# A gated delta-rule layer with a Hadamard FFN: output-weight folding moved from GpSimd to VectorE, split Horner tiles, and new instruction orders

## The reference, cut to what matters

```
xn = layernorm(x)
qkvz = xn @ w_qkvz.T ; q, k, v through a causal convolution of 4 taps ; b, a = xn @ w_ba.T
g = -exp(A_log) * softplus(a + dt_bias) ; beta = sigmoid(b) ; q, k normalised
for each token t:                       # 32 heads of 64
    S = S * exp(g_t) ; delta = (v_t - k_t S) * beta_t ; S = S + k_t delta^T ; o_t = q_t S
o = o * rsqrt(mean(o^2) + eps) * norm_weight * sigmoid(z) ; y_attn = o @ w_out.T
h = fwht(xn * SU_ug) ; u = silu(h @ W_gate.T * s_g) * (h @ W_up.T * s_u)
y_ffn = (fwht(u * SU_dp)) @ W_down.T * Wscale_dp        # fwht of length 1024
out = x + y_attn + y_ffn
```

## Time and profile before

| | |
|---|---|
| median of 3 runs | 920.72 us (919.37 to 922.29) |
| the profiled execution | 921.86 us, span 920.0 us |
| PE busy | 845.0 us (92%), 13354 products and as many weight loads |
| DVE busy | 703.3 us (76%) |
| ACT busy | 256.0 us (28%) |
| POOL busy | 287.7 us (31%) |
| mean granted PE clock | 0.967 of full speed |
| DMA | 49.56 MB, mean 54 GB/s |

### The profile page before, as it was taken

The page is one execution under the profiler, slowest core; times in us unless marked ns, Lnnn a source line. Parts: engine busy times, 40 slices in busy tenths (PEclk is TensorE's granted clock), DMA queues, the critical chain, the costliest instruction groups (busy, mean ns, idle before and its releaser), DMA issues.

```text
span 920.0 us, 30578 instructions
## 1 busy us (share of the span) xinstructions
PE 845.0 (92%) x13354; PEld 607.2 (66%) x13354; DVE 703.3 (76%) x1248; ACT 256.0 (28%) x560; POOL 287.7 (31%) x194
## 2 busy tenths in 40 slices
PE   1887499999999999999999999999999999998685
PEld 1533267766767676767676677767777767767574
DVE  5675968888887979788887878797978888795522
...
GB/s 124 128 58 81 6 77 36 31 82 30 94 30 83 23 80 37 69 32 64 60 31 82 30 94 24 89 19 77 42 58 44 41 84 30 60 31 14 30 2 46
DMA packets 129157, 49.56 MB, mean 54 GB/s; under 512 B 110977, under 2 KB 120449, under 8 KB 128897
## 3 DMA queue, kind: packets, MB, share of 16 engines
...
...
## 4 chain that ended last, share of the span: by engine, by line
PE 60%; DVE 17%; SPq 7%; DMA 6%; POOL 5%; issue 3%; ACT 1%; POOLq 0%; DVEq 0%; ACTq 0%
PE bank L581 17%; DVE kq L224 4%; PE bank L645 4%; PE bank L593 3%; PE bank L747 3%; SPq L512 3%; PE bank L662 3%; PE bank L749 3%; PE bank L692 3%; PE bank L602 3%; PE bank L664 3%; PE bank L730 2%; PE bank L668 2%; PE bank L719 2%; PE bank L678 2%
## 5 line engine op out<-in xcount | busy, mean ns | idle before, releaser
L581 PE MATMUL bank<-xnT,wq 128*128 128x512 f32 x512 | 261.8, 636 | 15.8 <-DVE kq L224 15.5
L224 DVE SCALAR_TENSOR_TENSOR kq<-bank,cw,kq 128x510 f32<-128x510 f32 (+2 forms) x288 | 214.6, 745 | 44.9 <-ACT kq L798 37.8
L581 PEld LDWEIGHTS bank<-xnT,wq 128*128 128x128 f32 x512 | 90.7, 195 | 98.1 <-issue 70.3
L948 POOL TENSOR_TENSOR ost<-ost,cst 128x8 f32<-128x8 f32 x32 | 52.3, 1634 | 191.7 <-DVE ost L357 191.7
L798 ACT ACTIVATE kq<-bank,cw 128x512 f32<-128x512 f32 x96 | 65.8, 685 | 143.3 <-PE bank L581 142.5
L944 POOL TENSOR_TENSOR Sd<-St,dec 128x256 f32<-128x256 f32 x32 | 19.9, 621 | 231.7 <-DVE St L345 161.4
L938 POOL TENSOR_TENSOR kqg<-kq,rows 128x1024 f32<-128x1024 f32 x32 | 75.5, 2358 | 39.0 <-DVE kq L224 39.0
L645 PE MATMUL bank<-kq 64*64 64x128 f32 x1024 | 69.0, 274 | 11.6 <-DVE kq L224 8.9
L911 POOL TENSOR_TENSOR kd<-kc,stat 128x512 f32<-128x512 f32 x32 | 33.4, 1042 | 144.1 <-DVE stat L261 144.1
L747 PE MATMUL bank<-wo,oT 128*128 128x256 f32 x256 | 70.6, 389 | 1.6 <-DVE oT L369 1.6
L270 DVE TENSOR_TENSOR ATP<-bank,gb 128x512 f32<-128x512 f32 x64 | 44.1, 689 | 30.4 <-issue 14.3
...
## 6 DMA issues: line engine op xcount, KB each, us to landing
rows<-decay_rows SPq DMA_DIRECT2D x64, 256.0 KB, 4.6
...
inverse_blocks<-UU SPq DMA_DIRECT2D x16, 256.0 KB, 2.0
...
wguT<-wgu_dram SPq DMA_DIRECT2D x8, 256.0 KB, 5.2
base_blocks<-ATP SPq DMA_DIRECT2D x128, 16.0 KB, 2.7
...
U<-inverse_blocks SPq DMA_DIRECT2D x128, 16.0 KB, 2.0
```

The source lines that it names most:

```text
L224: nc.vector.scalar_tensor_tensor(out=y[:, :, t:S], in0=p[:, :, 0:S - t], scalar=cw[:, m, i // 2, 3 - t:4 - t], in1=y[:, :, t:S], op0=ALU.m ...
L581: last = nc.tensor.matmul(ring[i % 2][:], wq[:, q, kc, i // 2, :], xnT[:, kc, (i % 2) * 512:(i % 2) * 512 + 512], start=kc == 0, stop=kc = ...
L948: nc.gpsimd.tensor_tensor(ost[:, 2, :], ost[:, 1, :], k("neghalf")[:, 0:B * 2], ALU.pow).then_inc(rms_done, 1)
```

## The change

1. **Folding.** `fold()` on POOL is gone. `W_down` is loaded early, as SP's fourth transfer, into a tile of its own (a view of `kqg`, which the pairs use later); `Wscale_dp` comes first on ACT's queue. DVE multiplies by `Wscale_dp` (`wscaled`, 2 instructions on 128x1024) and does the three butterfly levels (6 instructions on 128x1024), all in the setup, ahead of PE's Hadamard product. The factor 1/sqrt(1024) goes into ACT's eviction of it. The first `out` waits for that eviction and not for the fold; POOL's first `kqg` waits until PE has read the tile.
2. **Clearings first.** POOL's four clearings stand ahead of its wait for the statistics.
3. **Small loads on ACT's queue.** `wsd`, `ah` (4 transfers) and `nwh` (2) are issued by ACT ahead of its first instruction.
4. **Horner by corner tiles.** `hz.1` multiplies only the two 32x32 diagonal corners of `Q` for each head (64 products of 32x32 by 48 columns for each pair, where there were 32 of 64x64 by 48); `hz.3` uses 64x32 of `Q` and writes 32 rows.
5. **New orders** on all engines and on SP's queue. `fload` stands ahead of `oload` in the setup.

```diff
-        wdT = xs
+        wds = [kqg[:, i].rearrange("p k u c -> p (k u c)").rearrange("p (i d) -> p i d", i=IT) for i in range(2)]
...
+                def butterfly(src, dst, h, t):
+
+                    s4, d4 = (w.rearrange("p (a t h) d -> p a t h d", t=2, h=h) for w in (src, dst))
+                    step(nc.vector.tensor_tensor(d4[:, :, t], s4[:, :, 0], s4[:, :, 1], (ALU.add, ALU.subtract)[t]))
+
+                def wscaled(i):
+
+                    step(nc.vector.tensor_tensor(wds[1][:, 4 * i:4 * i + 4], wds[0][:, 4 * i:4 * i + 4], wsd[:].unsqueeze(1).broadcast_to([P, 4, HID]), ALU.mult))
+
+                dve.wait_ge(wdn_in, 16)
+                dve.wait_ge(wsd_in, 16)
+                wscaled(0)
                 dve.wait_ge(sq_done, TT)
                 step(nc.vector.tensor_scalar(st[:, 0, :], st[:, 2, :], 1.0 / HID, LN_EPS, ALU.mult, ALU.add))
                 steps["var"] = count[0]
+                wscaled(1)
                 dve.wait_ge(rstd_done, 1)
...
                 for q in (1, 3):
+                    butterfly(wds[1], wds[0], 1, q // 2)
                     dve.wait_ge(xnT_ready, q + 1)
...
+                for t in range(2):
+                    butterfly(wds[0], wds[1], 2, t)
+                for t in range(2):
+                    butterfly(wds[1], wds[0], 4, t)
+                steps["fold"] = count[0]
...
DVE's order
-K.out.0 K.turn.1 K.out.1 M.e M.stats K.out.2 K.out.3 M.gram.0 L.hz.0.0 L.hz.0.1 M.gram.1 M.vtr.0 L.hz.1.0 L.hz.1.1
-M.gram.2 L.hz.2.0 L.hz.2.1 M.ff M.gram.3 L.hz.3.0 L.hz.3.1 A.proj.0 L.state.0 M.vtr.1 L.ks.1 A.proj.1 M.inv.0 L.state.1
-A.proj.2 L.ks.2 M.inv.1 L.norm.0 L.state.2 A.proj.3 L.ks.3 L.gated.0 M.inv.2 L.turn.0 L.norm.1 A.proj.4 L.gated.1
-A.proj.5
+M.hz.3.0 M.hz.3.1 A.vtr.1 P.proj.0 M.state.0 P.proj.1 M.ks.1 A.inv.0 P.proj.2 M.state.1 A.inv.1 M.ks.2 M.norm.0
+P.proj.3 M.state.2 M.gated.0 M.ks.3 A.inv.2 M.turn.0 P.proj.4 M.norm.1 P.proj.5 M.gated.1 M.out.0 M.turn.1 P.e P.stats
+M.out.1 M.out.2 P.gram.0 M.out.3 P.gram.1 A.hz.0.0 P.vtr.0 A.hz.0.1 A.hz.1.0 P.gram.2 A.hz.1.1 P.ff A.hz.2.0 A.hz.2.1
+P.gram.3
...
SP's order
-M.rload M.fload L.bout L.bin A.load L.uout L.uin L.oload
+K.bin L.rload M.load L.fload K.oload K.uout K.uin L.bout
...
PE, hz.1
+                        if j == 1:
+                            for rs, cs in ((top, slice(0, H2)), (low, slice(H2, C))):
+                                for h in range(2):
+                                    last = nc.tensor.matmul(M[H][rs[h], i * n:i * n + n], Q[rs[h], u, cs], U16[rs[h], u, C - n:C], start=True, stop=True)
+                            continue
...
PE, hz.3
-                                last = nc.tensor.matmul(M[H][hs[h], i * n + n - H2:i * n + n], Q[hs[h], u, :], X[hs[h], q, u, H2:C], start=True, stop=True)
+                                last = nc.tensor.matmul(M[H][top[h], i * n + n - H2:i * n + n], Q[hs[h], u, 0:H2], X[hs[h], q, u, H2:C], start=True, stop=True)
...
PE's order
-M.proj.4 K.ks.3 M.ktr.1 K.delta.3 K.turn.0 K.o.1 M.proj.5 K.out.0 K.out.1 M.proj.6 M.vtr.0 K.turn.1 M.proj.7 K.out.2
-K.out.3 M.ff L.hz.0.0 L.hz.0.1 M.gram.1 L.hz.1.0 L.hz.1.1 M.gram.2 L.hz.2.0 L.hz.2.1 M.gram.3 L.hz.3.0 L.hz.3.1
-A.proj.0 L.delta.0 M.vtr.1 L.state.0 A.proj.1 L.ks.1 M.qsq L.delta.1 A.proj.2 L.state.1 L.o.0 L.ks.2 A.proj.3 L.delta.2
-A.ktr.0 L.state.2 A.gram.0
+K.hz.1.0 L.gram.2 K.hz.1.1 K.hz.2.0 L.gram.3 K.hz.2.1 L.vtr.1 K.hz.3.0 K.hz.3.1 M.proj.0 K.delta.0 M.proj.1 K.state.0
+L.qsq K.ks.1 M.proj.2 K.delta.1 M.proj.3 K.state.1 K.o.0 M.ktr.0 K.ks.2 M.proj.4 K.delta.2 M.ktr.1 K.state.2 M.gram.0
+K.ks.3 K.turn.0 K.delta.3 M.proj.5 K.o.1 K.out.0 K.out.1 M.vtr.0 M.proj.6 K.turn.1 M.proj.7 K.out.2 M.ff K.out.3
+M.gram.1 L.hz.0.0 L.hz.0.1
...
ACT's order
-A.ktr.0 L.delta.3 A.proj.4 A.ktr.1 L.norm.1 A.proj.5 M.inv.2 A.proj.6 A.proj.7 A.ff A.qsq P.proj.0 M.delta.0 P.proj.1
-M.oload M.delta.1 A.qsum P.proj.2 M.norm.0 M.delta.2 P.proj.3 P.dec
+K.delta.2 M.proj.4 M.ktr.1 K.delta.3 L.inv.2 M.proj.5 K.norm.1 M.proj.6 M.proj.7 M.ff A.proj.0 M.qsq L.delta.0 A.proj.1
+A.proj.2 M.qsum L.delta.1 M.oload A.proj.3 L.norm.0 A.dec A.ktr.0
...
POOL's order
-P.kqg.0 P.kd.0 P.gb.0 P.root P.gb.1 P.kqg.1 A.sd.1 P.kd.1 A.sd.2 A.norm.0 A.norm.1
+A.gb.1 A.kd.0 A.kqg.0 A.kqg.1 M.sd.1 M.sd.2 A.kd.1 M.norm.0 M.norm.1 P.gb.0 P.root
```

More of the change, by code:

```diff
@@ L458, in _ @@
                 program({"proj": proj, "ff": ff, "e": e, "stats": stats, "gram": gram, "vtr": vtr, "inv": inv, "hz": hz, "ks": ks,
-                         "state": state, "norm": norm, "gated": gated, "turn": turn, "out": out}, """K.out.0 K.turn.1 K.out.1 M.e M.stats K.out.2 K.out.3 M.gram.0 L.hz.0.0 L.hz.0.1 M.gram.1 M.vtr.0 L.hz.1.0 L.hz.1.1
-                         M.gram.2 L.hz.2.0 L.hz.2.1 M.ff M.gram.3 L.hz.3.0 L.hz.3.1 A.proj.0 L.state.0 M.vtr.1 L.ks.1 A.proj.1 M.inv.0 L.state.1
-                         A.proj.2 L.ks.2 M.inv.1 L.norm.0 L.state.2 A.proj.3 L.ks.3 L.gated.0 M.inv.2 L.turn.0 L.norm.1 A.proj.4 L.gated.1
-                         A.proj.5""")
+                         "state": state, "norm": norm, "gated": gated, "turn": turn, "out": out}, """M.hz.3.0 M.hz.3.1 A.vtr.1 P.proj.0 M.state.0 P.proj.1 M.ks.1 A.inv.0 P.proj.2 M.state.1 A.inv.1 M.ks.2 M.norm.0
+                         P.proj.3 M.state.2 M.gated.0 M.ks.3 A.inv.2 M.turn.0 P.proj.4 M.norm.1 P.proj.5 M.gated.1 M.out.0 M.turn.1 P.e P.stats
+                         M.out.1 M.out.2 P.gram.0 M.out.3 P.gram.1 A.hz.0.0 P.vtr.0 A.hz.0.1 A.hz.1.0 P.gram.2 A.hz.1.1 P.ff A.hz.2.0 A.hz.2.1
+                         P.gram.3""")
                 dve.wait_ge(acc_done, PAIRS * 4)
@@ L545, in _ @@
                 sp.dma_start(cst[:, 0:at], consts[:, 0:at]).then_inc(const_in, 16)
+                sp.dma_start(wds[0], wdown).then_inc(wdn_in, 16)
                 sp.dma_start(wbas[:], wba).then_inc(gate_in, 16)
[L547 to L549 removed]
                 for v, src in ((su, su_ug), (sd_, su_dp), (wsu, ws_up), (wsg, ws_gate)):
@@ L662, in hz @@
                                 last = nc.tensor.matmul(dst, ATP[hs[h], q, u, 0, :], T16[hs[h], u, 0:n], start=True, stop=True)
-                            elif j == 1:
-                                last = nc.tensor.matmul(dst, Q[hs[h], u, :], U16[hs[h], u, C - n:C], start=True, stop=True)
                             elif j == 2:
@@ L773, in _ @@
                     last.then_inc(xh_ready, 1)
[L774 removed]
+                pe.wait_ge(v_step, steps["fold"])
                 for m in range(4):
                     pe.wait_ge(xh_done, m + 1)
[L777 removed]
+                    nc.tensor.matmul(spare[m][:], k("had"), wds[0][:, 2 * m:2 * m + 2, :], start=True, stop=True).then_inc(wd_ready, 1)
                 program({"proj": proj, "ff": ff, "ktr": ktr, "vtr": vtr, "qsq": qsq, "gram": gram, "hz": hz, "ks": ks, "delta": delta,
[L779 to L782 removed]
+                         "state": state, "o": o, "turn": turn, "out": out}, """K.hz.1.0 L.gram.2 K.hz.1.1 K.hz.2.0 L.gram.3 K.hz.2.1 L.vtr.1 K.hz.3.0 K.hz.3.1 M.proj.0 K.delta.0 M.proj.1 K.state.0
+                         L.qsq K.ks.1 M.proj.2 K.delta.1 M.proj.3 K.state.1 K.o.0 M.ktr.0 K.ks.2 M.proj.4 K.delta.2 M.ktr.1 K.state.2 M.gram.0
+                         K.ks.3 K.turn.0 K.delta.3 M.proj.5 K.o.1 K.out.0 K.out.1 M.vtr.0 M.proj.6 K.turn.1 M.proj.7 K.out.2 M.ff K.out.3
+                         M.gram.1 L.hz.0.0 L.hz.0.1""")
             @block.scalar
```

61 lines of the change are left out of this document (21 added, 40 removed).

## The result

The changed kernel takes 960.2 us (median of 4 runs, 956.0 to 969.4), the kernel before, run beside it, 920.8 (4 runs, 919.4 to 922.3): ratio 1.0441, interval 1.0363 to 1.052. I had forecast 933, with 908 to 945 as the range. The direction was right, the size missed by 27 us.

The account below looks back on a forecast made before the run. PE's own instruction sequence was taken to set the steady-state time: 921.9 - 2.0 - 15.5 + 14 x (0.96 + 1.0) + 3 = 934.8 us profiled, 933.7 by the runs, stated as 933; range 908 to 945.

Parts of the forecast that it names:

- Part 1: Setup: pair 0 begins 2 us earlier through faster normalising, 2 of 4 us charged for work ahead; bounds -4 and 0.
- Part 2: Filling up to pair 1's FFN product: -15.5 us, from earlier block stores and DVE products no longer stalled; bounds -17 and -11.
- the 12.5 us of stalled products: Filling: DVE's products of two SBUF operands, standing still while POOL folds, would give back 12.5 us.
- Part 3: PE's instruction sequence in the steady state: +0.96 us for each pair, 14 times, from shape changes, `hz.3` and `hz.1`.
- The shape changes: PE's sequence: nine more changes of tile shape a pair, 31 for 22, at 0.10 us each, +0.9 us.
- `hz.3` (-0.8): PE's sequence: 64x32 products should cost like 32x32, 1.13 us for 32 instead of 1.93, -0.8 us a pair.
- `hz.1`: PE's sequence: 64 corner products at 0.042 us take 2.7 us for 1.85 before, +0.86 a pair; bounds 2.1 and 3.7.
- Part 4: PE's waits for each pair: +0.3 at `turn.1`, +1.2 from a DVE-POOL collision, -0.5 old waits, together +1.0 us.
- The collision of `inv.1` with POOL: Steady state: DVE's SBUF products fall under POOL's pair and lose about 1.55 us, of which about 1.2 reach PE.
- rival A: Steady state: the DVE-POOL collision stays in DVE's room; period 51.0, time 916.8, faster than before; chance 0.33.
- Part 5: Tail after the last periods: +3 us, +1.8 from later `gram.3` and +1.2 from Horner steps; bounds 0 and +6.
- C: Rival on `hz.1`: four-corner products cost more, 0.058 us each, giving 947 us; chance 0.05.

Follow-up runs that it names:

- e1: Changed kernel, but SP's queue issues the output weights' load (`oload`) one period earlier, after `uin`; 925.4 us, ratio 1.0046.
- e5: Changed kernel with the output weights' load issued earlier on SP's queue and the old `hz.1` and `hz.3`; 917.2 us, ratio 0.9971.
- e3: Changed kernel with `hz.1` and `hz.3` of the kernel before; 937.1 us, ratio 1.0157.
- e12: Kernel before with the new setup and 64x32 `hz.3`, `wscaled` and first butterfly level moved behind the copies of `xnT`; 903.7 us, ratio 0.9836.
- e9: Kernel before with the new setup alone, all orders and Horner steps old; 910.3 us, ratio 0.9882.
- e13: Kernel before with the new setup and 64x32 `hz.3`, `bout` and `bin` put first on SP's queue; 899.2 us, ratio 0.9779.
- e6: Kernel before with only the 64x32 form of `hz.3`; 910.9 us, ratio 0.9901.
- e4: Kernel before with both new Horner steps, `hz.1` and `hz.3`, alone; 938.6 us, ratio 1.0173.
- e7: Kernel before with only the four-corner form of `hz.1`; 940.5 us, ratio 1.0219.

## Why the prediction missed

**What bounds the kernel.** Right: PE's sequence sets the period, and the sum splits as I had split it. e1, e5 and the kernel before part the 3.39 us a period: 53.63 - 51.58 = 2.05 late weights, 51.58 - 51.07 = 0.51 corner tiles, 51.07 - 50.24 = 0.83 order. The first two aren't additive: from the changed kernel, taking the corner tiles back first (e3, by its fastest run) gives 1.81, and the load then 0.75.

**Part 1, setup, -2.0.** Wrong by about 3: pair 0's FFN product comes at 67.70, where it came at 66.92 before, +0.8. (Over all traces it comes at 64.3 to 66.9 with the old setup and at 65.6 to 68.6 with the new one, 1.7 later in the mean.) The normalising fell to 2.67 us, but the first half of `x` landed at 6.93 (before: at 4.73), and I charged 2 us for what stands ahead of the variance where DVE's wait for `W_down` alone was 3.78. By e12 even that was off the path: the last folding steps, which I had put under the wait for the gates, delay the gates themselves.

**Part 2, filling, -15.5.** Right in size, 15.48. Of its two halves, the 12.5 us of stalled products can have given no more than the 10 of e9, of which part is the clock: over these 208 products PE is busy 35.5 us before and 32.7 in e9, at a mean granted clock of 0.78 and 0.85. That the stores' place on SP's queue gives 5 is not borne out: e13 has it in the old order without the gain. The other 5 are shorter waits of PE and a higher granted clock, as e9's rows show; what in the new order brings them stays open.

**Part 3, sequence, +0.96.** The shape changes (+0.9 for nine) are right in kind: the traces have 22 a period before and 31 after, as counted. e5 has only six of the nine and +0.83 a period with no more waiting, where 0.10 for each would make 0.6. `hz.3` (-0.8) is right: its group fell by 0.80, of which, with one more edge, 0.6 reaches the period in e6. `hz.1` is the mis-sized term. I reasoned that the first of a float32 product's two instructions must end before the second begins in that tile, 42 ns for both; they take 25.6, so 1.6 us a pair instead of 2.7, below my lower bound of 2.1. The term is -0.2 (twice 0.82 for 1.85; in e4's order, 1.49 for both halves, it is -0.4) and not +0.86. The 25 ns for each instruction that I had worked out from the Trainium skill, "TensorEngine Tiling (Array Packing)", section Instruction Overhead, lie further off still: the rows have 12.8. Then the same speed cost more than it gave, by a mechanism that I hadn't got: PE goes on with a new block of instructions only 2.2 to 3.6 us after its transfer starts, and 128 fast products don't last that long. The corner form of `hz.1` costs 1.2 us a period in the old order (e7); both new steps together cost 0.5 in the new one (e1 against e5).

**Part 4, waits, +1.0.** This step failed, on both sides. The collision of `inv.1` with POOL is there, but half as large:

```profile
L310 DVE TENSOR_TENSOR prod<-UU,part 128x64 f32<-128x64 f32 x14 | 6.6, 474 | 0.5
L306 DVE TENSOR_TENSOR prod<-UU 128x64 f32<-128x64 f32 x14 | 6.1, 434 | 0.2
```

That is DVE of the kernel after, 300 to 700 us, by shape; before, the means were 271 and 263 ns. Four such products a pair make 0.75 us, not 1.55. I had charged DVE with the whole length of POOL's two instructions; it loses only where they lie beside products of two SBUF operands, and its reduction between them (L308) doesn't suffer:

```profile
511.76 0.90 DVE L306 TENSOR_TENSOR prod<-UU 128x64 f32<-128x64 f32 x2
511.93 0.62 POOL L952 TENSOR_TENSOR Sd<-St,dec 128x256 f32<-128x256 f32 x1 [6.15 <-DVE St L348]
512.70 0.29 DVE L308 TENSOR_REDUCE part<-prod 128x32 f32<-128x128 f32 x1
```

And in e5, which has the same collision (475 and 434 ns), PE never waits for `state` from 300 to 736 us: DVE's room takes it, as rival A had it (in e1 it waits so twice, 1.1 us in all). In its place stood a wait that I had not looked for. I had gone through the moved steps of DVE, PE and POOL, but of `oload` I had only noted that `fload` stands ahead of it in the setup. It moved on SP's queue, behind `rload` and `load`, and on ACT, one pair earlier in its use and ahead of `proj.3`. Both strings were in the diff. This made 2.05 us a period, or 28.7 of the 34.1 us between the two profiled executions (by the medians, 35 of 39); up to 0.6 of the 2.05 is the lower clock behind the waits, six stretches for one in e1 (an estimate: five times 1.7 us over 14 periods).

**Part 5, tail, +3.** +1.4, within the bounds.

**The rivals.** None named either cause. C had the corner products too slow, and they were too fast. A's mechanism (the collision is absorbed) is what happened, and with the load in time (e1) and the old Horner steps (e5) its time of 916.8 is met by 917.2. That the figures agree so well is luck: e5 lacks the two Horner terms of A's sum, which cancel in it (-0.8 and +0.86), and its shape changes cost what A gave to nine.
